# Rounded halves of a split softmax made on ScalarE and VectorE, low parts on GpSimd

## What is computed

```python
x = x + _L0_attn_ref(_layernorm(x), ...)
x = x + _L0_xattn_ref(_layernorm(x), ctx_768, Wq, Wk, Wv, Wo, bo)
x = x + _L0_ffn_ref(_layernorm(x), ...)

def _L0_xattn_ref(x, context, Wq, Wk, Wv, Wo, bo):       # 16 heads of 64
    q = (x @ Wq).reshape(B, Nq, 16, 64).transpose(0, 2, 1, 3)
    k = (context @ Wk).reshape(B, Nc, 16, 64).transpose(0, 2, 1, 3)
    v = (context @ Wv).reshape(B, Nc, 16, 64).transpose(0, 2, 1, 3)
    attn = softmax(einsum('bhid,bhjd->bhij', q, k) * 64 ** -0.5)
    out = einsum('bhij,bhjd->bhid', attn, v)
    return out.transpose(0, 2, 1, 3).reshape(B, Nq, 1024) @ Wo + bo
```

## Time and profile before

| | us |
|---|---|
| median of 3 runs (2865.43 to 2868.12) | 2867.56 |
| the profiled execution | 2871.38 |
| its span, first to last instruction | 2870.1 |
| VectorE busy | 2558.9 |
| TensorE busy | 2330.6 |
| GpSimd busy | 1514.1 |
| ScalarE busy | 1481.6 |

### The profile page before, as it was taken

The page is one execution under the profiler, slowest core; times in us unless marked ns, Lnnn a source line. Parts: engine busy times, 40 slices in busy tenths (PEclk is TensorE's granted clock), DMA queues, the critical chain, the costliest instruction groups (busy, mean ns, idle before and its releaser), DMA issues.

```text
span 2870.1 us, 55744 instructions
## 1 busy us (share of the span) xinstructions
PE 2330.6 (81%) x22188; PEld 1667.7 (58%) x22188; DVE 2558.9 (89%) x3360; ACT 1481.6 (52%) x2406; POOL 1514.1 (53%) x1220
## 2 busy tenths in 40 slices
PE   4778788887888888788888888888788787888885
PEld 3455565565656556566555655656566555665653
DVE  3799898998989899898998979899898998989994
ACT  2443555455554545555455454645556455565661
POOL 2254646454464645646464564645646455464692
PEclk8799999998999999899998989999899998999996
DMA  3000000000000000000000000000000000000000
GB/s 106 9 1 1 10 1 10 1 1 10 1 10 1 6 6 2 11 1 16 1 2 10 1 10 1 9 5 7 10 1 10 1 2 10 1 3 1 7 1 8
DMA packets 16721, 22.06 MB, mean 8 GB/s; under 512 B 4992, under 2 KB 14352, under 8 KB 16464
## 3 DMA queue, kind: packets, MB, share of 16 engines
q1 hardware_dynamic: 16464, 18.50, 2.0%
HBM read 16.27 MB, written 2.10 MB: 6 GB/s over the span
## 4 chain that ended last, share of the span: by engine, by line
DVE 47%; PE 27%; issue 13%; POOL 10%; ACT 4%; DMA 0%; SPq 0%; DVEq 0%; POOLq 0%; ACTq 0%
DVE pmax L917 20%; DVE EL L911 16%; POOL EH L1284 6%; PE PS L449 5%; PE PS L450 4%; PE PS L481 4%; PE PS L464 4%; PE PS L466 3%; DVE AL L925 2%; POOL Cf L1288 2%; PE PS L501 2%; PE PS L491 1%; ACT AH L762 1%; DVE X L884 1%; ACT PF L740 1%
## 5 line engine op out<-in xcount | busy, mean ns | idle before, releaser
L740 ACT ACTIVATE PF<-PS,s_scale 124x512 f32<-124x512 f32 x1664 | 1131.0, 686 | 933.6 <-PE PS L450 824.5
L1284 POOL CAST EH<-PF 124x1024 f16<-124x1024 f32 x832 | 1128.2, 1370 | 861.6 <-ACT PF L740 860.7
L911 DVE SCALAR_TENSOR_TENSOR EL<-EH,PF 124x1024 f16<-124x1024 f16 x832 | 1215.1, 1474 | 61.4 <-issue 33.5
L917 DVE TENSOR_REDUCE pmax<-PS 128x1 f32<-128x806 f32 x1024 | 991.3, 986 | 21.9 <-PE PS L481 21.2
L464 PE MATMUL PS<-Ch,EH 123*128 123x97 f16 (+1 forms) x6656 | 816.0, 213 | 85.5 <-DVE EL L911 72.4
L466 PE MATMUL PS<-Cl,EL 123*128 123x97 f16 (+1 forms) x6656 | 811.5, 212 | 0.0
L464 PEld LDWEIGHTS PS<-Ch,EH 123*128 123x128 f16 (+1 forms) x6656 | 635.6, 101 | 290.5 <-issue 158.7
L481 PE MATMUL PS<-ChT,AH 96*128 96x403 f16 x2048 | 545.1, 350 | 272.4 <-DVE pmax L917 256.7
L466 PEld LDWEIGHTS PS<-Cl,EL 123*128 123x128 f16 (+1 forms) x6656 | 624.7, 101 | 199.5 <-issue 36.7
L449 PE MATMUL PS<-AH,ChT 97*124 97x512 f16 x1664 | 678.6, 408 | 57.8 <-ACT PF L740 54.9
L450 PE MATMUL PS<-AL,ClT 96*124 96x512 f16 x1664 | 666.1, 400 | 0.0
(11 more groups left out here) (215 smaller groups left out, 1513.6 us busy)
## 6 DMA issues: line engine op xcount, KB each, us to landing
Cf<-in_ctx SPq DMA_DIRECT2D x16, 599.6 KB
X<-in_x SPq DMA_DIRECT2D x16, 128.0 KB, 4.1
out_x<-X SPq DMA_DIRECT2D x16, 128.0 KB, 1.7
msk<-in_attention_mask SPq DMA_DIRECT2D x4, 256.0 KB, 4.3
xWqT<-in_xWqT SPq DMA_DIRECT2D x2, 256.0 KB, 5.4
...
```

The source lines that it names most:

```text
L740: act.activation(PF[:, n % PRING, :], PS[0:KP, 4 + n % 2, :], ACT.Exp, scale=s_scale[0:KP, b % 4:b % 4 + 1]).then_inc(sg("ex"), 1)
L911: dve.scalar_tensor_tensor(out=EL[:, r - 1:r + 1, :], in0=EH[:, r - 1:r + 1, :], scalar=-KEEP, in1=PF[:, f - 1:f + 1, :], op0=ALU.mult, op ...
L917: dve.tensor_reduce(pmax[:, b % 2, ht, half:half + 1], PS[:, 2 * half:2 * half + 2, 0:NKEY], AX_XY, ALU.max).then_inc(sg("max_rd"), 1)
L1284: pool.tensor_copy(EH[:, r - 1:r + 1, :], PF[:, f - 1:f + 1, :]).then_inc(sg("eh"), 1)
```

## The change

- Rounding PF to EH leaves GpSimd. A new step `round` stands `ROUND_LAG` = 2 tiles behind the exponentials; ScalarE does the even pairs and VectorE the odd ones, 416 each. The factor KEEP goes into this rounding, and the low part becomes a plain subtraction, EL = PF - EH.
- The low part of one pair in four stays on VectorE (208), three in four go to GpSimd (624). The waits of `av` and of the exponentials follow: `rounded(p)` and `lowered(p)` name the semaphore and the count for pair p.
- The exponentials have no scale. The scale goes into the self attention's normed result (`sa_f`, now scaled by `u_scale`), into `sigma`, and into the copy to UT, which has `u_scale` now. `tau` and its chain go, and so does the scaling of `rden_u` (L935).
- The same for the queries: AH is made with KEEP on ScalarE, AL by a plain subtraction on VectorE.
- The context: `ctx_rest` on GpSimd goes; `ctx_hi` stays on ScalarE, and `ctx_lo` moves from ScalarE to VectorE, from Ch and Cf in one instruction.

```diff
+ROUND_LAG = 2
 def context_of(b):
-    return [(k, b, x) for k in ("ctx_hi", "ctx_rest", "ctx_lo") for x in range(2)]
+    return [(k, b, x) for k in ("ctx_hi", "ctx_lo") for x in range(2)]
...
+        if n % 2 and ROUND_LAG <= n < TOTAL + ROUND_LAG:
+            out.append(("round", n // 2 - ROUND_LAG // 2))
         if n % 2 and LO_LAG <= n < TOTAL + LO_LAG:
             out.append(("lo", n // 2 - LO_LAG // 2))
...
+        def rounded(p):
+            return sg("eh_act" if p % 2 == 0 else "eh_dve"), p // 2 + 1
+        def lowered(p):
+            return (sg("lo_dve"), p // 4 + 1) if p % 4 == 0 else (sg("lo_pool"), p // 4 * 3 + p % 4)
...
 # TensorE, step av
-                    w.wait_ge(sg("eh"), n // 2 + 1)
+                    w.wait_ge(*rounded(n // 2))
+                    w.wait_ge(*lowered(n // 2))
...
 # ScalarE
-                    w.wait_ge(sg("sigma"), b + 1)
                     w.wait_ge(sg("st"), n + 1)
                     if n >= PRING:
-                        w.wait_ge(sg("lo"), (n - PRING) // 2 + 1)
-                    act.activation(PF[:, n % PRING, :], PS[0:KP, 4 + n % 2, :], ACT.Exp,
-                                   scale=s_scale[0:KP, b % 4:b % 4 + 1]).then_inc(sg("ex"), 1)
+                        w.wait_ge(*lowered((n - PRING) // 2))
+                    act.activation(PF[:, n % PRING, :], PS[0:KP, 4 + n % 2, :], ACT.Exp).then_inc(sg("ex"), 1)
+                elif k == "round" and s.a[0] % 2 == 0:
+                    n = 2 * s.a[0] + 1
+                    f, r = n % PRING, n % ERING
+                    w.wait_ge(sg("ex"), n + 1)
+                    if n >= ERING:
+                        w.wait_ge(sg("av"), n - ERING + 1)
+                    act.activation(EH[:, r - 1:r + 1, :], PF[:, f - 1:f + 1, :], ACT.Copy,
+                                   scale=KEEP).then_inc(sg("eh_act"), 1)
...
 # VectorE
-                if k == "lo":
+                if k == "round" and s.a[0] % 2:
                     n = 2 * s.a[0] + 1
                     f, r = n % PRING, n % ERING
                     w.wait_ge(sg("ex"), n + 1)
-                    w.wait_ge(sg("eh"), n // 2 + 1)
                     if n >= ERING:
                         w.wait_ge(sg("av"), n - ERING + 1)
-                    dve.scalar_tensor_tensor(out=EL[:, r - 1:r + 1, :], in0=EH[:, r - 1:r + 1, :], scalar=-KEEP,
-                                             in1=PF[:, f - 1:f + 1, :], op0=ALU.mult,
-                                             op1=ALU.add).then_inc(sg("lo"), 1)
+                    dve.tensor_scalar(EH[:, r - 1:r + 1, :], PF[:, f - 1:f + 1, :], KEEP, None,
+                                      ALU.mult).then_inc(sg("eh_dve"), 1)
+                elif k == "lo" and s.a[0] % 4 == 0:
...
+                    dve.tensor_tensor(EL[:, r - 1:r + 1, :], PF[:, f - 1:f + 1, :], EH[:, r - 1:r + 1, :],
+                                      ALU.subtract).then_inc(sg("lo_dve"), 1)
...
-                    dve.scalar_tensor_tensor(out=AL[b % 2][:, cs], in0=AH[b % 2][0:DC, cs], scalar=-KEEP,
-                                             in1=PS[0:DC, 7, :], op0=ALU.mult, op1=ALU.add).then_inc(sg("q_lo"), 1)
+                    dve.tensor_tensor(AL[b % 2][:, cs], PS[0:DC, 7, :], AH[b % 2][0:DC, cs],
+                                      ALU.subtract).then_inc(sg("q_lo"), 1)
...
+                elif k == "ctx_lo":
...
+                    dve.scalar_tensor_tensor(out=Cl[b % 2][:, HALVES[x], 0:DC], in0=Ch[b % 2][:, HALVES[x], 0:DC],
+                                             scalar=-KEEP / REST, in1=Cf[:, HALVES[x], :], op0=ALU.mult,
+                                             op1=ALU.add).then_inc(sg("c_split"), 1)
...
 # GpSimd
-                        pool.tensor_copy(EH[:, r - 1:r + 1, :], PF[:, f - 1:f + 1, :]).then_inc(sg("eh"), 1)
-                elif k == "ctx_rest":
...
+                elif k == "lo" and s.a[0] % 4:
...
+                    pool.tensor_tensor(EL[:, r - 1:r + 1, :], PF[:, f - 1:f + 1, :], EH[:, r - 1:r + 1, :],
+                                       ALU.subtract).then_inc(sg("lo_pool"), 1)
```

112 lines of the change are left out of this document (45 added, 67 removed).

## The result

The changed kernel takes 2702.6 us (median of 4 runs, 2701.3 to 2704.3), the kernel before, run beside it on the same chip, 2866.5 us (2865.0 to 2868.1). The ratio is 0.9428, with a 95% interval from 0.9412 to 0.9445: 164 us less, where the prediction said 267 less and a range from 2420 to 2770. The sign and the range held. The forecast's own bounds, 2510 to 2690, were missed by 13 us and the size by 103, and the reasons for that are what the experiments are about. One execution of a later kernel (both reorderings together) ran in a slower state, at a granted clock of 0.737, and took 2884.2 us; it is left out of that kernel's median.

The account below looks back on a forecast made before the run. VectorE was taken to bound the kernel (2558.9 of 2870.1 us), with TensorE near. From the profiled 2871.4 us, 258 for 15 batches and 4 to reach the median were taken off: 2609, said as 2600, range 2420 to 2770.

Parts of the forecast that it names:

- The 258 us of the stretches: Whole kernel: 17.2 us less per batch, summed over four stretches of one batch's trace, for 15 batches.
- The rounding on VectorE, 0.75 us: VectorE's 416 new roundings of 1024 elements: 0.75 us each, extended from shorter instructions, 312 us together.
- EL by plain subtraction, 1.15 us: VectorE's 208 remaining low parts: 1.15 us each as plain subtraction instead of 1.219, 239 us together.
- `ctx_lo`, 0.8 us each, 26 us: The context's low part, moved to VectorE: 32 instructions of 0.8 us or less, 26 us together.
- The new waits, 302 + 30 us: VectorE waiting for GpSimd on the shared port: 302 us at roundings, some 30 at other SBUF instructions.
- VectorE after, 2190: VectorE's busy time after the change, waits included: 2190 us, 370 less.
- The second stretch, -1.5 us: Batch stretch of 13.2 us bound by GpSimd's casts and context split: only 1.5 us less, the shared port staying full.
- The last stretch, -15.8 us: Batch stretch of 147.6 us, 40 pairs of tiles, bound by VectorE: 132 us after the change, 15.8 less.
- Rival 4: Nothing moves: VectorE's saved work returns as waits for GpSimd's low parts, with three tiles of lead; chance 0.03.
- Rival 1: TensorE becomes the bound because VectorE waits 159 us for GpSimd, not 302: 2400 to 2510 us; chance 0.17.
- Rival 2: Dearer port or rounding on VectorE, which again sets the last stretch: 2690 to 2860 us; chance 0.22.
- Rival 3: Slower than before: VectorE's roundings always start just behind GpSimd's subtractions, each waiting more than 0.9 us; chance 0.08.

Follow-up runs that it names:

- both reorderings together: Changed kernel with GpSimd's low parts two tiles earlier in its list and no `max` steps at tiles 37 to 41 of a batch: 2624.9 us, ratio 0.9155.
- the fastest kernel: Changed kernel with GpSimd's low parts earlier, `max` steps moved off tiles 37-41, self-attention norm one tile earlier, ScalarE rounding two pairs of three: 2585.6 us.

## Why the prediction was right in sign and too large

**What bounds the kernel.** Right: VectorE bound the kernel before. With VectorE at 92 to 93% of the span small parts paid nearly in full (41 us for 53.5), and 319 us more load than in the kernel after cost 62, net of the stalls for GpSimd's low parts that went with it.

**The sum, by parts.** The 258 us of the stretches were some 42 for the scaling of `rden_u` and AL (2.8 a batch), 28 for the second and third stretch, where the split goes, and the remaining 188 for the new placement. Measured: 41, 61 and 56. So the placement alone missed by some 130 us, and that the whole missed by 103 is in part luck: the split was worth twice what was counted.

**The rounding on VectorE, 0.75 us.** 0.690 at the median. The step from instructions of 1, 32 and 128 elements to 1024 held to 9%.

**EL by plain subtraction, 1.15 us, and AL 65 ns less.** Wrong, and small: 1.218 at the median, as the three-operand form of before (1.219), and AL takes 686 ns. I had taken the 65 ns from two lines of another shape and with PSUM operands. 208 x 0.068 is 14 us.

**`ctx_lo`, 0.8 us each, 26 us.** The row of the kernel after, for the second half of each context:

```profile
L970 DVE SCALAR_TENSOR_TENSOR Cl<-Ch,Cf 124x576 f16<-124x576 f16 x16 | 39.1, 2441 | 0.0
```

2.44 us for 576 elements is mostly a wait for GpSimd's subtraction (with casts on GpSimd, as the split alone has them, it is 1.48); the other half takes 1.13. Together 57 us where 26 were counted.

**The new waits, 302 + 30 us, and nothing for the 208 EL.** The roundings wait 0.544 us in the mean (1.234 - 0.690), 226 us, where I had 0.726; the low parts, which I had excused, wait 0.248, 52 us. The sum, 278, is near. That a low part right behind a rounding goes unhindered was wrong: the rule that I used (the port had just been VectorE's) has no row behind it. The Trainium skill's rule ("SBUF — State Buffer", "Who interferes with whom"), that a `tensor_tensor` with two SBUF inputs and a fast `tensor_scalar` both have to wait for a whole instruction of GpSimd, is borne out by both lines: their longest cases, 2.668 and 3.145 us, are their shortest and most of a subtraction of 2.13.

**VectorE after, 2190.** 2214.7, off by 1%; the errors above nearly cancel.

**GpSimd's subtraction, 2.2 us; exponentials 0.59; roundings on ScalarE 1.05; ScalarE at most 1760.** 2.132, 0.597, 1.051 and 1683 us. ScalarE's roundings were costed at nothing. For the exponentials that held: TensorE's wait for PF fell to 14.6 us. But ScalarE's copy `U` stands behind them too, and TensorE waits for it 31.6 us where it was 9.1. That wait follows the number of ScalarE's roundings: 8.9 us with none (the old placement with the old instructions), 59.8 with 832. Some 23 us of waiting were left out of the sum. GpSimd was forecast at 1850 and is at 1753.

**The second stretch, -1.5 us.** The gain was 2.8, and the split alone gives 4.8 there with casts and low parts as they were, of which 1.5 come back in the third. I had argued from the shared port that eight pairs want as much time as today whatever happens to the split. But the work on the port was less than the sum of the single times: the seven casts of the earlier trace rows, with the EL among them, took 1.84 us a pair and not the 2.26 that I used, and with the split gone the first two stretches take 15.0 us (6.6 and 8.4), not 18. What held the second stretch was GpSimd's list, full for 13.09 of 13.2 us with the split's two subtractions in it, and ScalarE's, where exponentials stood behind `Cl` copies that waited for these: a queue as below, overlooked in a stretch where I had the chain of it in hand. The new placement then takes 2.3 us of it back.

**The last stretch, -15.8 us: the step that failed.** It said that with the old 7.5 us of idle time the stretch would take 128.3, and that 132 allowed for two engines near each other. The work came down as forecast (115.5 us; I had 120.8). The stretch took 139.8. The old idle time was no constant to be carried over: when VectorE is behind on everything it is never short of work, and the others' delays hide behind it. With VectorE at 83% of the stretch, every wait in the lists shows, and two large ones did: 3.1 us of TensorE for low parts that GpSimd had time to make, and 6.6 us at the selection, each with two tiles at TensorE's lower clock behind it. The second was there before and stayed; the first is new. The order with GpSimd's low parts ahead, with the same instructions, takes the first away and gives 94 us. That this is near the missing 103 is chance as far as batch 8 goes: there the new order brings the last stretch down by 3.9 us only, to 135.9, where 132 was forecast and 139.8 came.

**Rival 4 was the mechanism, and I put it off by a mean.** It said that the work comes back as waits for GpSimd's low parts, with three tiles of lead, and I gave it 0.03 because it "needs GpSimd at 100% in every stretch". It doesn't. GpSimd at 65% has 459 us of idle time right before its low parts in one page row, and part of it is time in which they were due. As it was written, with nothing gained, the rival did not happen; as a share of the result it is the 94 us. Rival 1 (TensorE as the bound) lies beyond: even the fastest kernel here has TensorE at 86%. Rival 2 gave the right time (2690 to 2860) for the wrong reason: the port was cheaper than I had it, not dearer. The range held only because half of this rival was in it. Rival 3 did not come: the rounding waits 0.54 us, and it would have had to wait over 0.9.

**What stays open.** In the fastest kernel TensorE still stands 14% of the span (it is busy 2224.9 of 2585.4 us), 104 us of it for `pmax`; which reordering would free the rest was not tried. How much of the 56 us of the placement is port and how much order was not taken apart either: the old placement was not run with another order.
